# Three graph attentions in one loop: max(row, column) weights in one float32 tile instead of two masks with high and low factors

## The reference

```python
# layer 1 (L1), "A" in the kernel; layer 3, "C", is the same with another W, a, and elu() on its result
Wh = jnp.einsum('bnf,of->bno', h, W)
s, t = Wh @ a[:Fo], Wh @ a[Fo:]
e = jax.nn.leaky_relu(s[:, :, None] + t[:, None, :], negative_slope=0.2)
alpha = jax.nn.softmax(jnp.where(adj == 0, -jnp.inf, e), axis=-1)
x = x + jnp.einsum('bnm,bmo->bno', alpha, Wh)
# layer 2, "B": e = leaky_relu(einsum('bid,bjd,dk->bkij', h, h, A)), picked by adj, softmax, times h
```

## Time and profile before

| | us |
|---|---|
| median of 3 runs | 1722.07 (1720.83 to 1725.84) |
| the profiled execution, its own time | 1729.38 |
| its span, first to last instruction | 1727.6 |
| TensorE busy | 1495.8 (87% of the span), 12740 matmuls |
| VectorE busy | 1323.3 (77%), 3869 instructions |
| ScalarE busy | 1190.0 (69%), 1841 instructions |
| GpSimd busy | 182.4 (11%) |
| mean granted TensorE clock | 0.952 of full speed |
| 16 DMA engines, mean in the attention loop | about a quarter busy |

### The profile page before, as it was taken

The page is one execution under the profiler, slowest core; times in us unless marked ns, Lnnn a source line. Parts: engine busy times, 40 slices in busy tenths (PEclk is TensorE's granted clock), DMA queues, the critical chain, the costliest instruction groups (busy, mean ns, idle before and its releaser), DMA issues. The chain is left out here.

```text
span 1727.6 us, 33849 instructions
## 1 busy us (share of the span) xinstructions
PE 1495.8 (87%) x12740; PEld 1205.6 (70%) x12740; DVE 1323.3 (77%) x3869; ACT 1190.0 (69%) x1841; POOL 182.4 (11%) x201
## 2 busy tenths in 40 slices
PE   3999996999456799999999999999999999999863
PEld 3999996555243676868768687686876868768652
DVE  3666663788356688989889898898998989987753
ACT  2777773222247778889788887888878888785841
POOL 3443320000000100000000000000000000000000
PEclk9999997999777899999999999999999999999976
DMA  9989972566412012222122221222222222111011
GB/s 191 209 197 207 200 159 76 180 242 246 147 49 74 24 57 69 73 62 60 58 80 74 62 58 60 80 74 62 56 62 80 74 62 56 50 56 50 13 30 33
DMA packets 108456, 162.03 MB, mean 94 GB/s; under 512 B 9344, under 2 KB 59136, under 8 KB 106240
## 3 DMA queue, kind: packets, MB, share of 16 engines
q1 hardware_dynamic: 85248, 117.86, 22.8%
q0 software_dynamic: 18432, 33.56, 10.5%
q10 hardware_dynamic: 4608, 8.39, 1.4%
HBM read 151.40 MB, written 41.94 MB: 112 GB/s over the span
## 5 line engine op out<-in xcount | busy, mean ns | idle before, releaser
L1283 PE MATMUL ps<-fac_A,mask_A 128*128 128x258 f16 x2048 | 243.5, 274 | 30.5 <-DVE agg L927 16.7
L1347 PE MATMUL ps<-hV,wts 128*128 128x129 f32 x2048 | 252.6, 279 | 11.4 <-DVE xC L959 4.9
L1283 PE MATMUL ps<-fac_C,mask_C 128*128 128x258 f16 x2048 | 237.7, 274 | 22.1 <-DVE mask_C L922 15.5
L1347 PEld LDWEIGHTS ps<-hV,wts 128*128 128x128 f32 x2048 | 241.2, 194 | 18.4 <-DVE xC L959 12.9
L1283 PEld LDWEIGHTS ps<-fac_A,mask_A 128*128 128x128 fp8e4 x2048 | 196.3, 98 | 72.5 <-DVE agg L927 28.6
L1283 PEld LDWEIGHTS ps<-fac_C,mask_C 128*128 128x128 fp8e4 x2048 | 196.6, 98 | 58.6 <-issue 10.0
L307 ACT ACTIVATE maskT<-ps 128x1024 fp8e4<-128x1024 bf16 x128 | 131.3, 1025 | 54.2 <-PE ps L341 42.2
L1185 ACT ACTIVATE lk<-ps 128x1024 f32<-128x1024 f32 x128 | 131.3, 1026 | 38.8 <-DVE wts L947 23.8
L947 DVE SCALAR_TENSOR_TENSOR wts<-lk,wts 128x1024 f32<-128x1024 f32 x128 | 154.4, 1218 | 2.3 <-ACT wts L1187 2.2
L1335 PE MATMUL ps<-g_hi,ag_hi 128*128 128x512 f16 x256 | 98.9, 386 | 51.4 <-ACT wts L1187 36.0
L1163 ACT ACTIVATE mask_A<-s_row,steep_t_A 128x1024 fp8e4<-128x1024 f32 x128 | 141.3, 1143 | 1.8
(11 more groups left out here) (240 smaller groups left out, 3226.8 us busy)
## 6 DMA issues: line engine op xcount, KB each, us to landing
adj_b<-in_adj POOLq DMA_DIRECT2D x128, 256.0 KB, 9.1
maskT_scratch<-maskT SPq DMA_DIRECT2D x16, 1024.0 KB, 6.8
ring_A<-maskT_scratch SPq DMA_DIRECT2D x64, 256.0 KB, 3.1
off<-maskT_scratch SPq DMA_DIRECT2D x32, 512.0 KB, 4.4
ring_C<-maskT_scratch SPq DMA_DIRECT2D x64, 256.0 KB, 3.6
xa<-in_x SPq DMA_DIRECT2D x16, 512.0 KB, 4.2
whT_scratch<-whT_s ACTq DMA_DIRECT2D x32, 256.0 KB, 6.5
whT_b<-whT_scratch SPq DMA_DIRECT2D x16, 512.0 KB, 4.7
```

What stands on the lines that cost most here:

```text
L1283: last = nc.tensor.matmul(Q_SLOTS[c % 2][:, k, 0:XW], m_fp8[x][:, k, j, c * P:c * P + P], fac[x][:, k, j, :], start=(j == 0), stop=(j == T ...
L1347: last = nc.tensor.matmul(Q_SLOTS[c // 2 % 2][:, c % 2, 0:PW], wts[:, j, c * P:c * P + P], hV[b % 2][:, j, :], start=(j == 0), stop=(j == ...
```

## The change

A and C get the weights of a softmax in one float32 tile. With `te` the row score less its maximum and `us` the column score plus that maximum, the weight over exp(te) is max(exp(0.8 us), exp(-0.8 te)), where exp(0.8 us) runs along the row and exp(-0.8 te) is one number for each partition. So:

- ScalarE makes `row_e` once per graph out of PSUM (`row_power`, two instructions), and `least` and exp(te) (`exps`, two small ones). `indicate`, `high`, `up` and `keep_s` go.
- VectorE's new `weights(x, b, j)` is one instruction per tile, 128x1024, `max` with `least` and `mult` with the edges in `ring`, eight per graph for A and for C. `make_below`, `make_above`, `low`, `gather`, `quotients` and the split copies go.
- The values times exp(te) are one float32 tile `hP`; A's are made by ScalarE (eight 128x128 instructions out of PSUM), C's by VectorE.
- TensorE's `attend` goes; `weigh` now serves A, B and C: 8 float32 matmuls of 129 columns for each c, two c to a slot.
- A's results are taken out of PSUM by `averages`, as B's; C's by `shares` on VectorE (the reciprocal) and `scaled` on ScalarE, which then frees the slot.
- B: ScalarE copies each `gram` result to SBUF (`keep_scores`), VectorE's `leaky` makes the leaky relu in place, ScalarE's `score_exps` is one exponential from SBUF to SBUF.
- C's relu out of PSUM moves from VectorE to ScalarE; `rows` is made from `us`, and so waits for the maximum; the order on VectorE, ScalarE and SyncE is written anew; one more bound is reduced at the end.

```diff
-                    def make_below(x, b, p):
-                        dve.wait_ge(S[x, "ring"][p % 2], (b * (PAIRS // 2) + p // 2 + 1) * 16)
-                        dve.wait_ge(S[x, "ind"], b * T + 2 * p + 2)
...
-                    def gather(x, b, c):
-                        dve.wait_ge(S[x, "up"], b * T + c + 1)
-                        nc.vector.scalar_tensor_tensor(agg[:, c, :], Q_SLOTS[c % 2][:, 1, 0:XW], ex[x][:, 3, c:c + 1], up_part[:, c % 2, :],
-                                                       ALU.mult, ALU.add).then_inc(S[x, "agg"], 1)
...
+                    def weights(x, b, j):
+
+                        if j % 2 == 0:
+                            dve.wait_ge(S[x, "ring"][j // 2 % 2], (b * (PAIRS // 2) + j // 4 + 1) * 16)
+                        if j == 0:
+                            dve.wait_ge(S[x, "exp"], b + 1)
+                            dve.wait_ge(S[x, "s_row"], 2 * b + 2)
+                        nc.vector.scalar_tensor_tensor(wts[x][:, j, :], row_e[x][:, :], least[x][:, j:j + 1], ring[x][:, j % MR, :],
+                                                       ALU.max, ALU.mult).then_inc(S[x, "wts"], 1)
+
+                    def leaky(b, j):
+                        dve.wait_ge(S["B", "kept"], b * T + j + 1)
+                        nc.vector.scalar_tensor_tensor(wts["B"][:, j, :], wts["B"][:, j, :], SLOPE, wts["B"][:, j, :], ALU.mult,
+                                                       ALU.max).then_inc(S["B", "lrelu"], 1)
...
+                    def averages(x, b, m, new, old):
+                        shares(x, b, m)
                         dve.drain()
                         for c in (2 * m, 2 * m + 1):
...
+                        for c in (2 * m, 2 * m + 1):
+                            last = nc.scalar.mul(quo[:, c, :], Q_SLOTS[m % 2][:, c % 2, 0:P], rec[x][:, c:c + 1])
+                        last.then_inc(S[x, "quo"], 1)
...
                         if b * PAIRS + p >= 2:
-                            sp.wait_ge(S[x, "mask"], b * PAIRS + p - 1)
+                            sp.wait_ge(S[x, "wts"], (b * PAIRS + p - 1) * 2)
...
-                    def attend(x, b, c):
-                        take(free_q, c % 2, S[x, "agg"], b * T + c + 1)
-                        if c == 0:
-                            pe.wait_ge(S[x, "fac"], 2 * b + 2)
-                        for k in range(2):
-                            for j in range(T):
...
+                    def weigh(x, b, c):
+
                         if c % 2 == 0:
-                            take(free_q, c // 2 % 2, S["B", "done"], b * (T // 2) + c // 2 + 1)
+                            take(free_q, c // 2 % 2, S[x, "quo" if x == "C" else "done"], b * PARTS + c // 2 + 1)
```

More of the change, by code:

```diff
@@ L753, in gnn_stack_kernel @@
             S["A", "q_in"], S["A", "x_in"], S["B", "ring"] = q_in, x_in, off_in
-            for n in ("quo", "quo_exp"):
-                S["C", n] = csem(f"C_{n}")
-            for n in ("var", "rstd", "shift", "h", "hT_made", "ahi", "lo", "off", "gram", "exps", "wts", "tile", "done"):
+            S["C", "quo_exp"] = csem("C_quo_exp")
+            for n in ("var", "rstd", "shift", "h", "hT_made", "ahi", "lo", "off", "gram", "kept", "lrelu", "exps", "tile", "rec", "quo", "done"):
                 S["B", n] = csem(f"B_{n}")
@@ L1044, in run @@
[L1044 to L1051 removed]
+                            factors("C", i - 2)
@@ new lines, in run @@
+                            weights("A", i + 1, 2)
+                        if GW:
+                            highest_share("B", 1)
+                            dve.drain()
+                            stats("C", newC, 0)
+                        if CA:
+                            shares("C", i - 2, 0)
+                        if GW:
+                            stats("C", newC, 1)
+                            moments("C")
+                        if nextA:
+                            weights("A", i + 1, 3)
@@ new lines, in run @@
+                        if CA:
+                            shares("C", i - 2, 1)
+                        if GW:
+                            shifts("C", i - 1)
+                        if AA:
+                            split_g(i)
+                            split_ag(i)
+                        if nextA:
+                            weights("A", i + 1, 4)
+                        if CA:
+                            shares("C", i - 2, 2)
+                        if AA:
+                            complement(i, 0)
+                            complement(i, 1)
@@ new lines, in keep_scores, with score_exps @@
+                    def keep_scores(b, j):
+                        act.wait_ge(S["B", "gram"], b * T + j + 1)
+                        if j == 0 and b > 0:
+                            act.wait_ge(S["B", "tile"], b * T)
+                        nc.scalar.copy(wts["B"][:, j, :], P_SLOTS[j % 2]).then_inc(S["B", "kept"], 1)
+                    def score_exps(b, j):
+                        act.wait_ge(S["B", "lrelu"], b * T + j + 1)
+                        nc.scalar.activation(wts["B"][:, j, :], wts["B"][:, j, :], ACT.Exp, bias=shiftB[:, 0:1]).then_inc(S["B", "exps"], 1)
@@ L1366, in run @@
                             if AA:
-                                attend("A", i, c)
+                                weigh("A", i, c)
                             if c == 0 and nextA:
```

551 lines of the change are left out of this document (233 added, 318 removed).

## The result

The changed kernel takes 1627.48 us, the median of four runs (1624.27 to 1629.24), against 1723.69 us for the kernel before in runs beside it: a ratio of 0.944, 95% interval 0.942 to 0.946. That is 96 us less, where the prediction said 115 and 1608 us. The time is inside the range of 1598 to 1650, and its direction and the main of its mechanism are right (TensorE's work unchanged, its waits gone), but the gain came out a sixth smaller than foretold. The time lies outside the 1598 to 1620 that the forecast itself had, and nearer to the first rival's 1636 than to 1608: the range holds because it was drawn to reach into that rival. The profiled execution took 1624.27 us with a span of 1622.5, so 105 us less than the profiled one of before.

The account below looks back on a forecast made before the run. TensorE was taken as nearest to its limit, with 66 us of work in a 72.1 us run and the rest waits. Terms (a) to (d) sum to -114.7 us, taking the median to 1607.4, said as 1608; range 1598 to 1650.

Parts of the forecast that it names:

- the first rival: Smaller TensorE waits come back in full runs: 28 us more, 1636 us; chance 24 of 100.
- TensorE: no change, 0 us: A's and C's matmuls become 128 float32 records starting at the same 0.112 us as before: 0 us.
- the second rival: Float32 weight loads on TensorE, 191 instead of 112 ns, become the limit: +20.2 us a run, 1931 us; 2 of 100.
- VectorE 53 to 55 us, ScalarE about 40: Busy time in a full run: VectorE falls from 64.6 to about 53 to 55 us, ScalarE from 60 to about 40.
- The u8 rival: The u8 operand slows VectorE's `weights` to 2.26 us each, making the kernel slower, 1744 us; chance 3 of 100.
- The waits go: TensorE's waits in a full run: the 2.5 us for ScalarE go, only 0.2 us lost in B's stretch.
- the walk: One full run followed step by step from the first gram: slots never late, 0.2 us lost in B's stretch, 66.1 us.
- (a): Eleven intervals from run 3 to run 14: a full run takes 66.4 us against 72.1, -62.6 us in all.
- (b): Filling the pipeline, up to `turn_q` of run 3: three intervals shorter by 6.2, 7.3 and 8.4 us.
- (c): From `turn_q` of run 14 to B's weighing in run 16: -12.0 us; B in run 16: -3.2 us.
- (d): Last chain, between the last two attends: 33.2 us instead of 45.5, -12.3; the end after it -3.0 and +0.3 us.
- The last rival: A bound breaks and the general path runs behind the loop: 2.8 ms more; chance 1 of 100.

Follow-up runs that it names:

- run 1: Not a follow-up: a pass of the kernel's own loop while the pipeline fills; no separate kernel or ratio.
- run 14: Not a follow-up: a loop pass whose `turn_q` ends the eleven full-run intervals, 67.04 us each in the changed kernel.
- run 16: Not a follow-up: a late loop pass, in which B has no A ahead of it; B's weighing takes 20.8 us in the changed kernel.
- run 3: Not a follow-up: the loop pass whose `turn_q` starts the eleven full-run intervals, 67.04 us each in the changed kernel.

## Why the prediction was right, and where it was off

**TensorE: no change, 0 us.** Right: added up over both traces, TensorE's work is the same. The spacing of A's and C's float32 `weigh` is 0.1116 us with loads of 192 ns, so the second rival (1931 us) is refuted. The Trainium skill ("TensorE: Matmul & The Clock Gate", section "Weight-path perf modes — Fast Weight Load (FWL) and DoubleRow") gives the fast weight load to types other than float32 only, at about twice the speed. The traces agree: 192 ns for a float32 load here, 97 for an fp8 one before.

**VectorE 53 to 55 us, ScalarE about 40.** 55.2 and 38.8. The terms given for VectorE add up to 52.3, not to 53 to 55. Of the 2.9 us between, 1 is `weights`, which was priced at 1.13 and follows at 1.19. The u8 rival is refuted twice over: the price of 1.28 us, and no change without the byte.

**The waits go.** Both of the earlier trace rows are gone. What took the 2.5 us away was not what the walk said, the earlier release of a slot: alone, that moves the waits to VectorE and gains nothing. The rest of the change, which relieves both engines (busy time a run down by 9 us on VectorE and 21 on ScalarE), saves 3.4 us a run without it, and takes the wait on the slot from 2.5 to 0.2. The earlier release is worth 1.7 us, but only on top of that. No run separates VectorE's relief from ScalarE's.

**(a) A full run, 66.4 against 67.04.** The failed step is the walk of B's stretch, where "A's maximum is back at 44.2 as `us`, `rows` wants it at 44.5". It has no place for `columns` of A standing behind `shifts` of B, and `shifts` behind a power that lasts 2.60 us beside `weights` and not 1.64. The loss is 1.3 us where the walk had 0.2: 0.27 at the maximum, 0.8 at the first half of the row, 0.15 at the second. The run without that loss was put 0.5 too high, at 66.2 against 65.73, and by luck this hid half of the miss. Eleven intervals at -5.05 are -55.6 us, against -62.6. The first rival, small waits in B's stretch, was right on the place, but it put 2.0 us a run where 0.6 came.

**(b) The fill: -16.7 against -21.9.** The three terms are 34.2, 55.4 and 132.2 us, against 33.5, 53.5 and 129.7 foretold. What failed was the reading of VectorE's order: g was taken to be split and the gram to follow, but `weights` 4 of A and `complement` stand between `ag_lo` and the first gram, 2.3 us in run 1. With the new order and the complement moved in these runs, the intervals up to run 1's end are 33.8, 54.2 and 62.9, where the prediction had 33.5, 53.5 and 63.3. Of what is left, the first interval has no B in it: 0.5 us are eight `weights` at 1.2 us and not at 1.13. In the second it is ScalarE, with B's normalising ahead of A's exponentials and row.

**(c) and (d) the end: -26.7 against -30.2.** From `turn_q` of run 14 to the weighing of B in run 16 are 128.0 us (125.9 foretold, of which 0.6 is the longer run), and that weighing takes 20.8 (19.3). Most of the 1.5 us is clock, which the sum left out: the 114 records behind the last exponential take 14.1 us, with a mean granted clock of 0.91, where 12.8 were counted. The long last chain, called the weakest term, came out at 33.5 us against 33.2. In it VectorE sets the pace, TensorE waiting for each `weights` in turn:

```profile
1581.06 0.80 PE L1309 MATMUL ps<-hP_C,wts_C 128*128 128x129 f32 x2 [0.34 <-DVE wts_C L884]
1582.25 0.80 PE L1309 MATMUL ps<-hP_C,wts_C 128*128 128x129 f32 x2 [0.40 <-DVE wts_C L884]
...
1585.27 0.80 PE L1309 MATMUL ps<-hP_C,wts_C 128*128 128x129 f32 x2 [1.02 <-DVE wts_C L884]
```

The 1.02 holds the wait for edges that was foretold. -55.6, -16.7 and -26.7 make -99.0 us from the first `turn_q` on. The difference to the 96 us of the medians is within what one execution differs from the next.

**The general path.** The last rival priced it at 2.8 ms. Where it ran, in the kernel with shortened sums, it took 17.7 ms, six times as much.

## What to carry to other kernels

A wait that the trace names is what ends last, not what the time hangs on: taking the 2.5 us of ScalarE away alone gained nothing (1.006), and a wait shown as 0.62 us gave back 1.3 when the order on VectorE was mended. Once an engine is within a per cent or two of its own work, look at the small steps of the engine beside it that stand behind a third engine's answer (here `columns` behind `shifts`), and put them ahead of it. An order that helps while the pipeline fills can cost in each full run; the two can be written apart.

## What the runs showed of the hardware

GpSimd's power of 128x8 numbers takes 1.64 us alone, 2.60 us when a 128x1024 `weights` of VectorE is already running as it starts (with a byte operand or without), and 1.64 when the `weights` starts 0.8 us or more into it. In the kernel before it took 1.64 for A and B and mostly 2.11 for C, where two 128x1024 `off` steps (line 942, int32) run beside it. A `scalar_tensor_tensor` of 128x1024 takes 1.28 us with a scalar per partition and 1.22 with a constant, whatever the order of its two operations and in place or not, and a one-byte second operand adds nothing. TensorE's granted clock was 1.00 in a full run of the kernel before, with 6.3 us of waits of 1.7 at most. In the runs with the doubled `weights` it was 0.95 to 0.98 on average and 0.50 behind a wait of 3.3 us.
